# Expert slots of a mixture-of-experts kernel laid out in half-slots of 64 rows, with 22 slots in place of 26

## The reference, cut to what matters

```python
shared = silu(x_flat @ shared_w1.T) @ shared_w2.T          # 256 -> 1024 -> 256
gate_logits = x_flat @ gate_w.T                            # 8 experts
top_k_gates, top_k_idx = top_k(gate_logits, 2)
top_k_gates = softmax(top_k_gates, axis=1)
gates = zeros((T, 8)).at[arange(T)[:, None], top_k_idx].set(top_k_gates)
h = einsum('td,ehd->teh', x_flat, experts_w1)
expert_out = einsum('teh,edh->ted', silu(h), experts_w2)
selected = einsum('ted,te->td', expert_out, gates)
return x + shared + selected                               # the residual is outside
```

## Time and profile before

| | |
|---|---|
| median of 3 runs | 326.29 us (326.14 to 326.43) |
| profiled execution, device time | 325.89 us |
| its span, first to last instruction | 324.0 us |
| TensorE busy | 306.7 us, 95% |
| weight loads busy | 259.6 us, 80% |
| DVE, ACT, POOL busy | 69%, 57%, 47% |
| mean granted TensorE clock | 0.996 of 2.4 GHz |

### The profile page before, as it was taken

How to read it: one execution, slowest core, us unless ns; L and a number is a source line. 1 busy time by engine, 2 the same in 40 slices (tenths; PEclk the granted TensorE clock), 3 DMA queues, 4 the chain that set the end, 5 groups by cost and what they waited for, 6 DMA issues and landing times.

```text
span 324.0 us, 9888 instructions
## 1 busy us (share of the span) xinstructions
PE 306.7 (95%) x3521; PEld 259.6 (80%) x3521; DVE 223.4 (69%) x502; ACT 184.5 (57%) x355; POOL 152.1 (47%) x208
## 2 busy tenths in 40 slices
PE   8789999999998999999999999999999999999990
PEld 6678788988777999999997777777787787777870
DVE  0637888888898989999886868755554546565530
ACT  1366768878896978476768878733232332323220
POOL 0577747777586322112622344656353544434131
PEclk9999999999999999999999999999999999999998
DMA  7775335322241117814798774243323242333121
GB/s 231 260 222 210 108 111 179 111 83 77 77 124 58 32 31 205 269 24 95 195 275 309 185 239 110 45 67 41 60 42 59 34 67 35 54 48 46 22 34 16
DMA packets 18642, 36.37 MB, mean 112 GB/s; under 512 B 3331, under 2 KB 10982, under 8 KB 18598
## 3 DMA queue, kind: packets, MB, share of 16 engines
q1 hardware_dynamic: 12166, 27.71, 26.2%
q0 software_dynamic: 6432, 8.03, 16.3%
HBM read 28.52 MB, written 7.21 MB: 110 GB/s over the span
## 4 chain that ended last, share of the span: by engine, by line
PE 76%; DVE 9%; DMA 4%; POOL 3%; issue 3%; ACT 2%; SPq 1%; POOLq 1%; DVEq 0%; ACTq 0%
PE bank L820 21%; PE bank L833 14%; PE bank L643 7%; PE bank L835 6%; PE bank L500 6%; PE bank L602 6%; DMA out_rows<-y,add_id 2%; PE bank L525 2%; PE bank L551 2%; DMA weights<-in_patches 2%; PE bank L591 2%; PE bank L565 1%; PE bank L555 1%; DVE weights L1309 1%; PE bank L453 1%
## 5 line engine op out<-in xcount | busy, mean ns | idle before, releaser
L820 PEld LDWEIGHTS bank<-x_t,weights 128*128 x1248 | 87.5, 98 | 25.5 <-issue 0.2
L820 PE MATMUL bank<-x_t,weights 128*128 128x128 f16 x1248 | 103.8, 219 | 0.0
L1002 ACT ACTIVATE act_out<-bank 128x512 f32<-128x512 f32 (+2 forms) x72 | 42.0, 585 | 86.1 <-PE bank L820 71.8
L1270 POOL DMA_INDIRECT out_rows<-y,add_id x26 | 43.0, 1653 | 69.6 <-DVE y L1626 48.1
L833 PE MATMUL bank<-weights,hid_hi 128*128 x192 | 73.3, 382 | 0.2
L1417 DVE SCALAR_TENSOR_TENSOR hid_lo<-act_out,hid_hi 128x512 f16<-128x512 f32 (+2 forms) x72 | 48.6, 680 | 12.5 <-ACT hid_hi L1013 11.0
L835 PE MATMUL bank<-weights,hid_lo 128*128 x192 | 52.3, 273 | 0.0
L1423 DVE SCALAR_TENSOR_TENSOR weights<-stage,weights 128x1024 f16<-128x1024 f32 x36 | 43.0, 1221 | 0.7 <-ACT weights L959 0.7
L959 ACT ACTIVATE weights<-stage 128x1024 f16<-128x1024 f32 x36 | 36.8, 1049 | 0.0
L1237 POOL DMA_INDIRECT slot_rows<-x_rows,gather_id x26 | 28.0, 1075 | 13.0 <-DMA out_rows<-y 5.2
L500 PE MATMUL bank<-weights 128*111 128x256 f32 x132 | 31.3, 386 | 1.6 <-DMA weights<-in_patches 1.1
(11 more groups left out here) (164 smaller groups left out, 522.8 us busy)
## 6 DMA issues: line engine op xcount, KB each, us to landing
stage<-in_w_ffn SPq DMA_DIRECT2D x36, 512.0 KB
weights<-in_patches SPq DMA_DIRECT2D x11, 333.0 KB, 3.3
x_rows<-rows SPq DMA_DIRECT2D x11, 111.0 KB
out_rows<-weights SPq DMA_DIRECT2D x10, 111.0 KB
out_rows<-y POOLq DMA_DIRECT2D x9, 119.0 KB, 5.3
weights<-in_w_embed SPq DMA_DIRECT2D x3, 256.0 KB, 4.2
stage<-in_w_qk SPq DMA_DIRECT2D x1, 512.0 KB, 6.9
slot_rows<-x_rows,gather_id POOLq DMA_INDIRECT x26, 4.1
```

The costliest lines, as they stand in the source:

```text
L820: mm = nc.tensor.matmul(o, weights[:, bass.ds(base + 2 * k * CHUNK + 2 * (col - col % D) + w * D + col % D, P)], x_t[:, b, (2 * x + k) * P ...
L1002: nc.scalar.activation(d_, s_, ACT.Silu, scale=1.0 / (X_SCALE * W_SCALE)).then_inc(hid_acted, 1)
L1270: nc.gpsimd.indirect_dma_start(out=out, out_offset=bass.IndirectOffsetOnAxis(ap=add_id[:, j:j + 1], axis=0), in_=y[:, y_place(j)], in_offs ...
```

## The change

Experts' rows are now counted in halves of 64. `SLOT_TILES` is (2*1184 + 8*64)//64//2 = 22. The first eight slots are pairs: rows 0 to 63 belong to one expert and rows 64 to 127 to another. The pairs 0 to 3 hold the first 64 rows of experts 1 to 8, so that their experts are constants. The pairs 4 to 7 hold what is left over in halves, and the 14 slots behind them hold 128 rows of one expert; the experts of both kinds are read on the chip. In a pair both products have the weights stationary and 64 token columns moving; the second product comes out turned, so ACT copies it to SBUF (`copy_y`), TensorE turns it back in fp32 (`turn_y`), and DVE scales each half by its own gate (`pair_y`). Each half has its own scatter of 64 rows. Chunks are split in another order (`CHUNK_ORDER`) and earlier, and three products of `fill_values` move from DVE to GpSimd (`fill_gates`).

```diff
-SLOT_TILES = (2 * TOKENS + EXPERTS * (P - 1)) // P
+HALF = P // 2
+SLOT_TILES = (2 * TOKENS + EXPERTS * HALF) // HALF // 2
+STATIC_PAIRS = EXPERTS // 2
+PAIRS = STATIC_PAIRS + EXPERTS // 2
+FULL = SLOT_TILES - PAIRS
+CHUNK_ORDER = (*range(20), 20, 24, 21, 25, 22, 26, 23, 27, 28, 32, 29, 33, 30, 34, 31, 35)
+UP_NEEDS = (10, 18, 24, 32)
+DOWN_NEEDS = ((12, 12), (20, 20), (26, 28), (34, 36))
...
-        LATE_SHARED = [0, 0, 0, 0, 1, 1, 1, 2, 2, 2]
-        LATE_SLOT = [2, 2, 2, 2, 2, 2, 2]
+        LATE_SHARED = [0, 0, 0, 0, 1, 1, 2, 2, 3, 3]
+        LATE_SLOT = [3, 3, 3, 2]
...
+                for a in range(2 * NT):
+                    mm = nc.tensor.matmul(bank[7][0:HALF, D:D + 5 * PAIRS].rearrange("p (a b) -> p a b", b=PAIRS),
+                                          in_row[0:T, a, HALF:], in_tile[0:T, a, :, 0:PAIRS],
                                           start=(a == 0), stop=(a == 2 * NT - 1))
...
+                if j < STATIC_PAIRS:
+                    base_of[j] = ((2 * j + 1) * EW, (2 * j + 2) * EW)
+                elif j < PAIRS:
+                    base_of[j] = (known(2 * (j - STATIC_PAIRS)), known(2 * (j - STATIC_PAIRS) + 1))
+                else:
+                    base_of[j] = known(j)
...
+            def up_pair(n, b, bases, c):
+                col = c * P
+                for half_ in range(2):
+                    o = bank[2 * b + c // 4][:, c % 4 * P + half_ * HALF:c % 4 * P + (half_ + 1) * HALF]
+                    for k in range(KC):
+                        for w, x in ((0, 0), (0, 1), (1, 0)):
+                            at = (2 * x + k) * P + half_ * HALF
+                            mm = nc.tensor.matmul(
+                                o, weights[:, bass.ds(bases[half_] + 2 * k * CHUNK + 2 * (col - col % D)
+                                                      + w * D + col % D, P)],
+                                x_t[:, b, at:at + HALF],
+                                start=(k == 0 and w + x == 0), stop=(k == 1 and w == 1))
...
+            def down_pair(n, b, bases, c):
+                if c % 4 == 0:
+                    pe.wait_ge(lo_ready, 2 * n + c // 4 + 1)
+                if c == 0:
+                    nc.tensor.matmul(bank[5 + b][:, 0:D], nothing, weights[:, 0:D], start=True, stop=False)
+                for half_ in range(2):
+                    at = bases[half_] + 2 * KC * CHUNK + c * 2 * D
+                    token = c * P + half_ * HALF
+                    for q in range(KC):
+                        for hid, w in ((hid_hi, 0), (hid_hi, 1), (hid_lo, 0)):
+                            mm = nc.tensor.matmul(
+                                bank[5 + b][:, q * P + half_ * HALF:q * P + (half_ + 1) * HALF],
+                                weights[:, bass.ds(at + w * D + q * P, P)], hid[:, b, token:token + HALF],
+                                start=False, stop=(c == HC - 1 and half_ == 1 and q == 1 and hid is hid_lo))
...
+            def turn_y(j):
+                pe.wait_ge(y_copied, j + 1)
...
+                for half_ in range(2):
+                    for q in range(KC):
+                        mm = nc.tensor.transpose(
+                            bank[7][0:HALF, half_ * D + q * P:half_ * D + (q + 1) * P],
+                            y_t[:, q * P + half_ * HALF:q * P + (half_ + 1) * HALF], id32)
...
                 for c in range(HC):
-                    up_chunk(n, b, P, this_expert, c)
+                    up_of(j, c)
+                    if c == 3 and 2 <= j < PAIRS + 2:
+                        turn_y(j - 2)
                     if c == 4 and j + 1 < SLOT_TILES:
                         rows_of(j + 1)
                         know(j + 1)
-                    if c == 0 and j <= EXPERTS:
-                        wait_split(pe, (j + 1) * CHUNKS)
-                    down_chunk(n - 1, 1 - b, P, last_expert, c)
+                    down_of(j - 1, c)
...
             for j in range(SLOT_TILES - 1):
+                if 2 <= j < PAIRS + 2:
+                    copy_y(j - 2)
                 silu_half(UNITS + j, P, 0)
...
+                if j < PAIRS:
+                    for half_, ids, src in ((0, add_id, y[0:HALF, y_place(j)]), (1, pair_id, y_b[0:HALF, j % 2])):
+                        pool.wait_ge(y_scaled, UNITS + 2 * j + half_ + 1)
+                        if 2 * j + half_:
+                            pool.wait_ge(added, 16 * (2 * j + half_))
+                        nc.gpsimd.indirect_dma_start(
+                            out=out, out_offset=bass.IndirectOffsetOnAxis(ap=ids[0:HALF, j:j + 1], axis=0),
+                            in_=src, in_offset=None, compute_op=ALU.add).then_inc(added, 16)
...
+            def pair_y(j):
+                dve.wait_ge(y_turned, j + 1)
...
+                if j >= 2:
+                    dve.wait_ge(added, 16 * scatters(j - 1))
```

More of the change, by code:

```diff
@@ L89, in build @@
         expert_of = sb("expert_of", [P, SLOT_TILES], I32)
+        pair_gate = sb("pair_gate", [P, PAIRS])
+        pair_id = sb("pair_id", [P, PAIRS], U32)
+        y_space = rows[:].rearrange("p a b -> p (a b)").bitcast(F32)
+        y_t = y_space[:, 0:D]
+        y_b = y_space[:, D:3 * D].rearrange("p (a b) -> p a b", b=D)
+        id32 = y_space[:, 3 * D:3 * D + P]
+        nothing = y_space[:, 3 * D + P:3 * D + P + HALF].bitcast(F16)
         qk_stage = stage[:, 4].rearrange("p (k d) -> p k d", k=KC)
@@ L321, in pair_of @@
         def pair_of(c, w):
-            both = weights[:, bass.ds(2 * CHUNK * c, 2 * CHUNK)]
+            both = weights[:, bass.ds(2 * CHUNK * CHUNK_ORDER[c], 2 * CHUNK)]
             return both.rearrange("p (g w d) -> p g w d", w=2, d=D)[:, :, w]
@@ L343, in y_place, with scatters @@
             return 2 if j == SLOT_TILES - 1 else j % 2
+        def scatters(slots):
+            return slots + min(slots, PAIRS)
         block = ctx.enter_context(nc.Block())
@@ new lines, in up_of, with down_of @@
+            def up_of(j, c):
+                if j < PAIRS:
+                    up_pair(UNITS + j, j % 2, base_of[j], c)
+                else:
+                    up_chunk(UNITS + j, j % 2, P, base_of[j], c)
+            def down_of(j, c):
+                if j < STATIC_PAIRS and c % 4 == 0:
+                    wait_split(pe, DOWN_NEEDS[j][c // 4])
+                if j < PAIRS:
+                    down_pair(UNITS + j, j % 2, base_of[j], c)
+                else:
+                    down_chunk(UNITS + j, j % 2, P, base_of[j], c)
@@ L1061, in drain_hi, with late_chunk, copy_y @@
                 split_hi(FRONT_CHUNKS + n)
-            def late_hi(n):
-                for c in late_at(n):
-                    if c == PATCH_CHUNK:
-                        act.wait_ge(experts_known, 1)
-                    if c == EXPERTS * CHUNKS:
-                        act.wait_ge(inverse_ready, 1)
-                    split_hi(c)
+            def late_chunk(c):
+                if c == first_in_patch:
+                    act.wait_ge(experts_known, 1)
+                if c == first_in_tables:
+                    act.wait_ge(inverse_ready, 1)
+                split_hi(c)
+            def copy_y(j):
+                act.wait_ge(y_ready, UNITS + j + 1)
+                if j:
+                    act.wait_ge(y_turned, j)
+                nc.scalar.copy(y_t, bank[5 + j % 2][:, 0:D]).then_inc(y_copied, 1)
+            def late_hi(n):
+                for c in late_at(n) if n < UNITS else late_at(n)[1:]:
+                    late_chunk(c)
             copy_prob_t(NT - 2)
@@ L1118, in _ @@
                         act.wait_ge(h2_stored[q], 16 * len(range(q, NT, 4)))
+                    for q in range(ROWS):
+                        act.wait_ge(rows_out[q], 16 * len(range(q, NT, ROWS)))
+                    act.wait_ge(x2_turned, NT)
+                    nc.scalar.copy(id32, s_id).then_inc(id32_ready, 1)
                 if n < UNITS - 1:
```

219 lines of the change are left out of this document (151 added, 68 removed).

## The result

The changed kernel takes 364.64 us (median of 4 runs, 364.35 to 365.21) against 326.33 us: ratio 1.1176, 95% interval 1.1162 to 1.1189. The forecast was 353.5, the range 345 to 367. The direction and the mechanism were right, and the size was 11.1 us short. The profiled execution took 364.45 us, its span is 362.5. A run more than 1.5% above the fastest of its kernel is not compared, which concerns two of the four runs of experiment 2 (338.10 and 338.46 us).

What follows compares the result with a forecast made beforehand. Computed weight places in TensorE's sequencer, uncovered in pairs 4 to 7, were to bound the kernel: +23.4 for the steps, +0.1, +0.9, +0.6, +2.2 made +27.2 on 325.89, so 353.1, median 353.5 us; range 345 to 367.

Steps and rivals of the forecast that it cites:

- the time up to slot 1: Routing, `inverse` and step 0 ahead of slot 1: +0.9, +0.6 and +0.1 us.
- what stands beside the computed places: Register loads, waits and transposes beside a dynamic step's rounds: 0.7 us in step 4, 0.6 in 5 to 7, 0.5 in 8.
- steps 4 to 9: Dynamic pairs and first full step: 10.1 for step 4, 49.8 for 5 to 7, 12.5 for 8, 6.1 for 9.
- B: Rival: the 672 narrow matmuls of steps 0 to 3 run at 50, not 29 ns: +14, 367.5 us; chance 0.12.
- E: Rival: clock falls in steps 5 to 7, a following full step runs slow, costing 3 to 6 us: 358; chance 0.08.
- Steps 1 to 3: Static pairs: 6.1 us for step 1, 6.6 each for 2 and 3; TensorE's wait for the low part adds 2.2.
- Price of a computed place: TensorE's sequencer needs 0.125 us per computed weight place, whether one or two matmuls hang on it.
- Steps 5 to 7: Dynamic pairs, `up` and `down` together: 16 places a round, 16.0 us plus 0.6 beside them, 16.6 each.
- Steps 10 to 20: Full slots as in the kernel before: 11 steps at 5.62 us, 61.8 us.
- the credit: Routing: three products (2.08 us) moved from DVE to idle GpSimd were to give back 2.1 us.
- D: Rival: `down_pair` computes the third product's place again, 4 us more in each of steps 5 to 8: 369.5; chance 0.06.
- C: Rival: places computed ahead at 46 ns, steps 4 to 8 fall to 33 us: 314, or 324 with scatters binding; chance 0.06.

Runs made afterwards that it cites:

- experiment 2: Changed kernel, low part's product in dynamic pairs reading the high part's place, 256 places fewer: 333.01 and 334.39 us. A second part added places to the kernel before: 379.01.
- experiment 4: Two weight places per register instruction: changed kernel, dynamic pairs only, 339.60 us; kernel before, `up` products, 322.10 us, repeated in five rounds 321.81 us.
- experiment 6: Changed kernel, two separate edits: gate products back on VectorE, 363.83 us; added routing operations put behind shared-unit work on VectorE, 363.76 us.
- experiment 6's first kernel: Changed kernel with the three gate products moved back from GpSimd to VectorE: 363.83 us, ratio 1.1164.
- experiment 4's changed kernel: Changed kernel with two weight places per register instruction in the dynamic pairs, 1088 to 832 instructions: 339.60 us, ratio 1.0394.
- experiment 2's second part: Kernel before, second `up` matmul of each three reading weights 4 bytes further on, so 416 more computed places: 379.01 us, ratio 1.1613.
- experiment 1: Changed kernel with fixed experts in pairs 4 to 7, so all pairs' places are constants (512 computed places go): 331.20 us, ratio 1.016.

## Why the prediction was right in kind and 11.1 us short

The mechanism holds: computed places that nothing covers bound pairs 4 to 7. Two terms of the sum were mis-sized. The larger is the time up to slot 1, where the sum had 1.6 us and 7.25 were measured (5.7 short). The other is what stands beside the computed places where the sequencer is the bound (4.5 short in steps 4 to 9). Steps 1 to 3 add 1.2, the rest cancels within 0.2. The errors of any size all have one sign. The measured 364.6 us lie above the forecast's own range of 346 to 361, and the stated range up to 367 takes them in by room that was left for B and E, whose costs did not come. That the number stayed inside it is in part luck.

- **Price of a computed place: right.** 0.125 us was forecast from 16 places under 24 matmuls. Removing 256 of them took 30 to 32 us off (31.7 by that price), and 0.97 to 1.08 us for a group of eight in the chain is what 8 x 0.125 says. Not foreseen: by the split of experiment 4, an estimate, the price belongs to the instruction (0.096) more than to the place (0.028).
- **Steps 5 to 7: 16.6 forecast, 17.75 measured.** 128 x 0.124 = 15.9 leaves 1.9 us beside the places, where I put 0.6 by an ordinary step, in which this lies under matmuls. By the starts of the register instructions 0.8 of the 1.9 stand around the two register loads, and 1.1 in fifteen gaps of 154 to 280 ns among the 128, where the others are 124. The same error was in experiment 2's expectation for the kernel before. Steps 4 to 9 together: 83.0 us from 197.97 to 280.98 against 78.5 forecast, +4.5. A register load in the record (duration in ns min/median/max):

```profile
L835 PEldq TENSOR_LOAD <-expert_of x22: 298/302/489, 197.2 to 342.3; - x22
```

- **Steps 1 to 3: 22.7 us from 175.22 to 197.97, against 21.5** with the wait of 2.2: +1.2. VectorE's six chunk splits stand ahead of the first slot's low part, as forecast, and TensorE then waited 1.93 us for it at 179.19. In the second step a chunk's transfer ends late (5.70 us in the chain, 172.79 to 178.49), where I had priced ACT and chunks at nothing. These are VectorE's timeline and the chain:

```profile
171.55 6.89 DVE L1569 SCALAR_TENSOR_TENSOR weights<-stage,weights 128x1024 f16<-128x1024 f32 x6
178.36 0.68 DVE L1563 SCALAR_TENSOR_TENSOR hid_lo<-act_out,hid_hi 128x512 f16<-128x512 f32 x1
```

```profile
172.79 5.70 DMA stage<-in_w_ffn
```

- **Steps 10 to 20**: 61.9 us against 61.8. Level.
- **Up to slot 1: +7.25 us, forecast 1.6.** `inverse` starts 5.1 us later (157.31 in the chain against 152.19) and lasts 1.11 + 0.80 in place of 1.39, +0.5 as forecast. The 5.1, where the sum had 0.9, consist of three parts:
  - About 0.6 us stand ahead of anything that the change touches: the last wait of TensorE for VectorE before the token counts ends at 128.75 us against 128.12. In the other profiled executions of the changed kernel and its variants it ends between 127.97 and 129.08, so this is a difference of executions.
  - About 3.4 us are VectorE's. `find_tiles` and `move_ranks` together took 5.2 us (133.44 to 137.05 and 137.62 to 139.19), as charged (5.0). What failed is the credit: the moved products were to give back 2.1 us, and beside them VectorE lost 2.4 (experiment 6). TensorE feels VectorE's delay as the wait of 2.65 us that ends at 142.51.
  - About 1.0 us is TensorE's clock. Behind that wait it was granted 0.50 from 143.6 to 147.0 us, and the 168 matmuls up to `inverse` took 14.6 us (142.51 to 157.15) where experiment 6's first kernel, at 1.00 there, needed 13.0 (141.87 to 154.84). Of these 1.7 us 1.0 shows, since VectorE's tables were not done until 156.0. Experiment 4's changed kernel, the same up to here, had the same wait and kept 1.00. Its `inverse` started at 156.07, held by the tables:

```profile
156.07 1.28 PE L746 MATMUL bank<-weights 111*128 111x110 f16 x22 [0.46 <-DVE weights L1784]
```

  So the 2.3 us between the changed kernel and experiment 6's first one at `inverse` are not the price of the products on GpSimd. Counted from the wait that ends at 128 us, experiment 4's changed kernel needs 27.4 us to `inverse` and experiment 6's first 26.7: 0.6 us, the theory's number. The remaining 1.6 us between `inverse` and slot 1's copy I did not take apart.
- **Rival B is refuted** by 0.35 us for twelve matmuls beside constant places. **D** by the count of 1088. **C** by the 0.97 to 1.08 us, and by experiment 2's second part, where its 46 ns a place would have left 326 us and 379 were measured.
- **Rival E: half right.** The clock did fall, as it said. Three windows of the changed kernel, in step 5, in steps 5 and 6, and from the end of step 8 into step 9 (us, busy time of each engine, granted clock, DMA share, GB/s):

```profile
215.20:222.10 6.90, 6.71 (x79) 5.78 (x78) 1.47 (x3) 1.81 (x3) 1.78 (x2) 0.51 0.17 31
225.50:239.10 13.60, 13.35 (x156) 11.64 (x155) 2.16 (x4) 3.10 (x6) 2.14 (x3) 0.50 0.09 17
270.00:280.00 10.00, 9.90 (x114) 7.90 (x114) 2.79 (x6) 1.90 (x4) 3.87 (x3) 1.00 0.17 30
```

  0.50 is half of the full clock, which the forecast calls 1.2 GHz; the views give the clock only as a share. It was granted for most of 215 to 266 us. But it cost little. From 239.1 to 242.5 us the granted clock was 1.00, and the groups of twelve take as long there as the 0.97 to 1.08 us above, at 0.50:

```profile
240.09 1.05 PE bank L884 x12
241.14 1.07 PE bank L903 x12
```

  That is the register instructions' own pace: their starts lie 124 ns apart at either level. Only the transposes are slower, 0.93 and 0.43 us for the two groups of a step where they take 0.50 and 0.22 at 1.00, at most 0.64 us in each of steps 5 to 7, and part of that is won back behind them. (Four transposes of 128 columns in 0.43 us are 54 ns for 64 columns; the forecast had 53 at this level.) From 270 to 280 us, before the full steps, the clock is back at 1.00. Rival E's price was that of a full step at the lower level, 3 to 6 us, and it did not come. With half the instructions in these pairs (experiment 4) the clock stays at 1.00 through all slots.

What the change bought, by experiment 1: with free addresses its 20 steps take 132.9 us (174.51 to 307.42) where 24 took 136.2. Four slots fewer are worth 3.3 us, and the routing that they need costs 6.5 up to slot 1 in that kernel. So it would have lost even without a register instruction in its pairs.

## What to carry to other kernels

Count the instructions that the engine's sequencer has to run, address arithmetic above all, and set their time against the work under which they lie: here five computed places in a round cost next to nothing under 0.66 us of matmuls, and sixteen were the bound over 0.70. A resource that is hidden by 5% is not hidden: here the matmul behind the register load took 0.35 us in place of 0.22, and a little slack bought there (two places asked for together) gave 1.2 to 1.5% on a kernel whose TensorE is 95% busy. When another engine seems to offer a free place for moved work, look at what the instructions of both take side by side before crediting the move.

## What the runs showed of the hardware that I had not expected

- TensorE's register instruction: 46 ns in the record with one place and 74 with two, but their starts about 124 and 152 ns apart, at granted clocks of 0.50 and 1.00 alike for the first.
- TensorE at a granted clock of 0.50 while busy for 13.35 of 13.60 us (225.5 to 239.1): in steps where its array had 24 matmuls of 64 columns in about 2 us, and back at 1.00 in the steps behind. Ahead of the slots it fell to 0.50 behind a wait of 2.65 us in the changed kernel and stayed at 1.00 behind one of 2.66 us in experiment 4's changed kernel, alike up to there.
- Loads of 128 columns kept up with matmuls of 64 columns at 29 ns each (0.35 us for twelve, at 189.17 us). One of 128 columns took 98 ns, one of 119 took 134.
- A scatter of 64 rows follows another in 3.9 us, one of 128 rows in 4.5: half the rows save 0.6 us.
